# mLSTM heads in pairs on TensorE, with four weight and decay buffers and a finish spread over two batches

## The reference

```python
h_in = rmsnorm(x, norm1_w)
q, k, v = heads(h_in @ wq), heads(h_in @ wk), heads(h_in @ wv)   # 8 heads, 16 / 16 / 32 features
o_pre = h_in @ w_og
i_pre, f_pre = soft_cap(h_in @ w_ig + b_ig), soft_cap(h_in @ w_fg + b_fg)
Fcum = cumsum(log_sigmoid(f_pre))
Dmat = where(causal, Fcum[s] - Fcum[t] + i_pre[t], -inf);  m = max_t(Dmat)
C = (q @ k.T / sqrt(16)) * exp(Dmat - m)
n = max(|sum_t C|, exp(-m));  h = (C / n) @ v                    # for each head
h_out = sigmoid(o_pre) * (h * rsqrt(mean(h * h) + eps) * mh_w)
x1 = x + h_out @ w_out
out = x1 + silu(rmsnorm(x1) @ w_gate) * (rmsnorm(x1) @ w_up) @ w_down
```

## Time and profile before

| | |
|---|---|
| median of three runs | 750.72 us |
| the profiled execution | 753.29 us |
| its span | 751.5 us |
| PE busy | 712.5 us (95%), mean granted clock 0.935 |
| DVE busy | 443.5 us (59%) |
| ACT busy | 423.5 us (56%) |
| POOL busy | 252.0 us (34%) |

### The profile page before, as it was taken

How to read it: one execution, slowest core, us unless ns; L and a number is a source line. 1 busy time by engine, 2 the same in 40 slices (tenths; PEclk the granted TensorE clock), 3 DMA queues, 4 the chain that set the end, 5 groups by cost and what they waited for, 6 DMA issues and landing times. The chain is left out here.

```text
span 751.5 us, 15356 instructions
## 1 busy us (share of the span) xinstructions
PE 712.5 (95%) x5290; PEld 670.3 (89%) x5290; DVE 443.5 (59%) x961; ACT 423.5 (56%) x1106; POOL 252.0 (34%) x265
## 2 busy tenths in 40 slices
PE   8999999999999999999987999988998799999995
PEld 8999999999999999999877999987666579999995
DVE  6465665576655766566565655643155437655686
ACT  5566686667756677666684333366454544333553
POOL 3624742244422434224741411217254122111011
PEclk9999999999999999999999999998556659999998
DMA  6266644456343663436500400007320100000000
GB/s 228 72 209 196 174 131 123 119 167 176 118 119 100 181 181 102 131 96 185 169 3 4 159 2 0 15 11 235 113 69 15 44 0 1 2 0 0 1 28 28
DMA packets 44889, 69.63 MB, mean 93 GB/s; under 512 B 3376, under 2 KB 30640, under 8 KB 44592
## 3 DMA queue, kind: packets, MB, share of 16 engines
q1 hardware_dynamic: 44416, 68.31, 30.4%
q10 hardware_dynamic: 432, 0.79, 0.3%
HBM read 52.18 MB, written 16.91 MB: 92 GB/s over the span
## 5 line engine op out<-in xcount | busy, mean ns | idle before, releaser
L303 PE MATMUL PJ<-xTh,WBh 128*128 128x256 f32 x364 | 106.6, 293 | 0.4 <-POOL WBl L808 0.4
L305 PE MATMUL PJ<-xTh,WBl 128*128 128x256 f32 x364 | 102.7, 282 | 0.0
L304 PE MATMUL PJ<-xTl,WBh 128*128 128x256 f32 x364 | 102.7, 282 | 0.0
L545 ACT ACTIVATE probs<-SC,nmax 128x256 f32<-128x256 f32 x128 | 59.5, 471 | 63.9 <-DVE nmax L671 62.4
L793 POOL TENSOR_TENSOR stage<-stage 128x256 f32<-128x256 f32 x32 | 24.5, 765 | 164.1 <-DVE stage L659 164.1
L669 DVE TENSOR_REDUCE rmax<-SC 128x2 f32<-128x512 f32 x64 | 44.2, 691 | 54.4 <-PE SC L384 47.5
L1154 PE MATMUL UG<-xTh,WBh 128*128 (+1 forms) x256 | 73.5, 287 | 1.1 <-PEq L49 1.1
L552 ACT ACTIVATE probs<-probs,rinv 128x256 f32<-128x256 f32 x128 | 58.5, 509 | 27.2 <-DVE rinv L675 27.1
L1157 PE MATMUL UG<-xTh,WBl 128*128 (+1 forms) x256 | 72.4, 283 | 0.0
L1155 PE MATMUL UG<-xTl,WBh 128*128 (+1 forms) x256 | 72.4, 283 | 0.0
L303 PEld LDWEIGHTS PJ<-xTh,WBh 128*128 128x128 f32 x364 | 69.2, 190 | 1.0 <-issue 0.6
(11 more groups left out here) (252 smaller groups left out, 2453.4 us busy)
## 6 DMA issues: line engine op xcount, KB each, us to landing
K<-scr_k SPq DMA_DIRECT2D x60, 256.0 KB, 4.5
raw<-in_w_att SPq DMA_DIRECT2D x37, 256.0 KB, 4.7
Q<-scr_q SPq DMA_DIRECT2D x15, 512.0 KB, 7.4
stage<-scr_m SPq DMA_DIRECT2D x4, 1024.0 KB, 5.9
scr_q<-rot_h SPq DMA_DIRECT2D x30, 128.0 KB
scr_q<-rot_l SPq DMA_DIRECT2D x30, 128.0 KB
scr_k<-rot_h SPq DMA_DIRECT2D x30, 128.0 KB
scr_k<-rot_l SPq DMA_DIRECT2D x30, 128.0 KB
```

The source lines that it names most:

```text
L303: pe.matmul(out, ah, bh, start=(i == 0), stop=False)
L304: pe.matmul(out, ah, bl, start=False, stop=False)
L305: last = pe.matmul(out, al, bh, start=False, stop=(i == n - 1))
L545: last = act.activation(probs[:, j % 2, t, :], SC[j % 2][:, t, :], ACT.Exp, scale=SCALE, bias=nmax[:, j % 2, t:t + 1], accum_out=rsum[:, j ...
```

## The change

- The loop over heads becomes a loop over pairs (`PAIRS`). PE issues the scores of two heads together, one pair ahead, across batches too, and then the values of two heads together.
- Decays and weights have four buffers each instead of two. The two new ones of each kind lie in `rows`, a tile that also holds the rows of the gates (`cumS`, `gr`, `nm`, `ones`, `M`), which are dead by then. The first values therefore wait for the last output gate. ACT runs four heads ahead of the weighing.
- `rows_T` goes ahead of the last projection, and `exp_nm` and the first four decays between the parts of the last evacuation. The mask of batch 0 is added by DVE in quarters of two heads (`mask_first`) instead of by POOL; two of them stand behind the first two weighings. All weight pieces of the feed-forward are split in batch 0, and SP loads them ahead of the rows of batch 2.
- The finish of batch c is spread over batches c + 1 (to `norm_b`) and c + 2 (`heads_T`, `project_out`, `add_heads`), the norm over c + 2 and c + 3. The rest goes into the first two batches of the feed-forward, whose second batch is written out for that (`finish_last`).
- The output gate is `tanh(o / 2)`, and `norm_b` multiplies by `1 + tanh(o / 2)`, twice the sigmoid. The factor 4 in `norm_a` takes the 2 back.

```diff
-        cumS, gr, M, nm, ones = (sb(n, [P, S]) for n in ("cumS", "gr", "M", "nm", "ones"))
+        rows = sb("rows", [P, 6 * S])
+        cumS, gr, nm, ones, M = (rows[:, i * S:(i + 1) * S] for i in range(5))
...
+        decay_buf = [ga[:, 0, :], ga[:, 1, :], rows[:, 768:1152], rows[:, 1152:1536]]
+        weight_buf = [gb[:, 0, :], gb[:, 1, :], rows[:, 0:384], rows[:, 384:768]]
...
+            if second_hook:
+                chunk(1, False)
+            with eng.Fori(2 if second_hook else 1, B) as c:
...
-        AT = dict(take=0, squares=2, norm_a=2, norm_b=4, heads_T=5, hoT_hi=7, hoT_lo=7, out=7,
-                  ssq=3, xs=3, T=4, hi=5)
-        MLP_PIECES = (3, 2, 2)
+        PAIRS = HM // 2
+        MLP_PIECES = (2, 2, 2, 1)
...
                 pe.wait_ge(s_["c_ready"], HM * c + h + 1)
+                if c == 0 and h == 0:
+                    pe.wait_ge(s_["og_ready"], TT * B)
                 if c or h >= 4:
                     pe.wait_ge(s_["vt_ready"], HM // 2 * c + h // 2 - 1)
-                w = gb[:, h % 2, :]
+                w = weight_buf[(HM * c + h) % 4]
...
-                scores(c, 0)
-                for h in range(HM):
-                    if h + 1 < HM:
-                        scores(c, h + 1)
-                    values(c, h)
-                    if h == 0 and c:
-                        back(c - 1, 3)
-                    if h in (2, 4, 6):
-                        back(c, h // 2 - 1)
-                    if h == AT["T"] and c >= 2:
-                        pe_T(pe, 2, c - 2)
-                    if h == AT["heads_T"] and c:
-                        heads_T(c - 1)
-                    if h == AT["out"] and c:
-                        project_out(c - 1)
+                if c == 0:
+                    scores(0, 0)
+                    scores(0, 1)
+                for pair in range(PAIRS):
+                    if pair + 1 < PAIRS:
+                        scores(c, 2 * pair + 2)
+                        scores(c, 2 * pair + 3)
+                    elif c + 1 < B:
+                        scores(c + 1, 0)
+                        scores(c + 1, 1)
+                    values(c, 2 * pair)
+                    values(c, 2 * pair + 1)
+                    if pair:
+                        back(c, pair - 1)
+                    elif c:
+                        back(c - 1, PAIRS - 1)
+                    if pair == 0 and c >= 2:
+                        heads_T(c - 2)
+                    if pair == 0 and c >= 3:
+                        pe_T(pe, 2, c - 3)
+                    if pair == 1 and c >= 2:
+                        project_out(c - 2)
...
             for c in range(1, B):
                 project(c)
-            rows_T()
+                if c == 2:
+                    rows_T()
             for c in range(B):
...
             def finish_heads(k, c, ht):
                 if ht == 0:
-                    back(3, 3)
+                    back(3, PAIRS - 1)
+                    heads_T(2)
+                if ht == 1:
+                    project_out(2)
+                    pe_T(pe, 2, 1)
+                if ht == 5:
+                    heads_T(3)
+                if ht == 6:
+                    project_out(3)
+                    pe_T(pe, 2, 2)
+            def finish_last(ht):
                 if ht == 2:
-                    pe_T(pe, 2, 2)
-                if ht == 4:
-                    heads_T(3)
-                if ht == 5:
-                    project_out(3)
-                if ht == 7:
                     pe_T(pe, 2, 3)
-            ffn_pe(pe, 1, finish_heads)
+            ffn_pe(pe, 1, finish_heads, finish_last)
...
-                    act.activation(og_v[:, c, t, :], UG[2 + t][:, D:2 * D], ACT.Sigmoid).then_inc(s_["og_ready"], 1)
+                    act.activation(og_v[:, c, t, :], UG[2 + t][:, D:2 * D], ACT.Tanh, scale=0.5).then_inc(s_["og_ready"], 1)
...
-                if h % 4 == 0:
-                    act.wait_ge(s_["masked"], 2 * c + h // 4 + 1)
-                if c or h >= 2:
-                    act.wait_ge(s_["c_ready"], HM * c + h - 1)
-                e, a, at = ga[:, h % 2, :], A[c % 2], 32 * c + h
+                if c == 0 and h % 2 == 0:
+                    act.wait_ge(s_["masked_first"], h // 2 + 1)
+                if c and h % 4 == 0:
+                    act.wait_ge(s_["masked"], 2 * (c - 1) + h // 4 + 1)
+                if c or h >= 4:
+                    act.wait_ge(s_["c_ready"], HM * c + h - 3)
+                e, a, at = decay_buf[(HM * c + h) % 4], A[c % 2], 32 * c + h
...
+            exp_nm()
             mlp_hi(4, 5)
-            evac(3)
-            exp_nm()
+            evac_qk(3)
+            decay(0, 0)
+            decay(0, 1)
+            evac_og(3)
+            decay(0, 2)
+            decay(0, 3)
             for c in range(B):
-                for h in range(HM):
-                    decay(c, h)
-                    if h == 0 and c:
-                        take_pair(c - 1, 3)
-                    if h in (3, 5, 7):
-                        take_pair(c, (h - 3) // 2)
-                    if h == AT["take"] and c:
+                for pair in range(PAIRS):
+                    if pair:
+                        take_pair(c, pair - 1)
+                    elif c:
+                        take_pair(c - 1, PAIRS - 1)
+                    if pair == 0 and c >= 2:
+                        hoT(c - 2)
+                    if pair == 0 and c >= 3:
+                        act_hi(act, 2, c - 3)
+                    if pair == 1 and c:
                         take(c - 1)
-                    if h == AT["squares"] and c:
                         squares(c - 1)
-                    if h == AT["ssq"] and c >= 2:
+                    if pair == 2 and c >= 2:
                         act_ssq(act, 2, c - 2)
-                    if h == AT["hi"] and c >= 2:
-                        act_hi(act, 2, c - 2)
-                    if h == AT["hoT_hi"] and c:
-                        hoT(c - 1)
-                    if c < 3 and h >= 8 - MLP_PIECES[c]:
-                        i = 5 + sum(MLP_PIECES[:c]) + h - 8 + MLP_PIECES[c]
-                        mlp_hi(i, i + 1)
-            take_pair(3, 3)
+                    if c == 0:
+                        i = RING + sum(MLP_PIECES[:pair])
+                        mlp_hi(i, i + MLP_PIECES[pair])
+                    for u in (HM * c + 2 * pair + 4, HM * c + 2 * pair + 5):
+                        if u < HM * B:
+                            decay(u // HM, u % HM)
...
+            def mask_first(quarter):
+                dve.wait_ge(a_in[0], 32)
+                a = A[0][:, 2 * quarter:2 * quarter + 2, :].rearrange("p h (b n) -> p h b n", n=P)[:, :, 0:3:2, :]
+                m = mask[:, :].rearrange("p (a b n) -> p a b n", a=1, b=1).broadcast_to([P, 2, 2, P])
+                dve.tensor_tensor(a, a, m, ALU.add).then_inc(s_["masked_first"], 1)
...
-                if c or h >= 2:
-                    dve.wait_ge(s_["pv_ready"], HM * c + h - 1)
-                dve.scalar_tensor_tensor(gb[:, h % 2, :], UG[h % 2][:, 0:384], 1.0 / math.sqrt(DQ), ga[:, h % 2, :],
+                u = HM * c + h
+                if u >= 4:
+                    dve.wait_ge(s_["pv_ready"], u - 3)
+                dve.scalar_tensor_tensor(weight_buf[u % 4], UG[h % 2][:, 0:384], 1.0 / math.sqrt(DQ), decay_buf[u % 4],
...
-                dve.tensor_tensor(ho[:, :, :], ho[:, :, :], og_v[:, c, :, :], ALU.mult).then_inc(s_["ho_ready"], 1)
+                dve.scalar_tensor_tensor(ho[:, :, :], og_v[:, c, :, :], 1.0, ho[:, :, :], ALU.add,
+                                         ALU.mult).then_inc(s_["ho_ready"], 1)
...
             split(1)
             split(2)
-            split(3)
             dve.wait_ge(s_["rows_ready"], 1)
             dve.tensor_copy(gcol[:, :, :], X[:, 0:S].rearrange("p (t h) -> p t h", t=TT)).then_inc(s_["gcol_ready"], 1)
+            split_qk(3)
+            mask_first(0)
+            take_v(3, 0)
+            mask_first(1)
+            take_v(3, 1)
             for c in range(B):
-                for h in range(HM):
-                    weigh(c, h)
-                    if h == AT["norm_a"] and c:
+                for pair in range(PAIRS):
+                    weigh(c, 2 * pair)
+                    weigh(c, 2 * pair + 1)
+                    if c == 0 and pair == 0:
+                        mask_first(2)
+                        mask_first(3)
+                    if pair == 0 and c >= 2:
+                        hoT(c - 2)
+                    if pair == 0 and c >= 3:
+                        dve_lo(dve, 2, c - 3)
+                    if pair == 1 and c:
                         norm_a(c - 1)
-                    if h == AT["xs"] and c >= 2:
+                    if pair == 2 and c >= 2:
+                        add_heads(c - 2)
+                    if pair == 3 and c:
+                        norm_b(c - 1)
+                    if pair == 3 and c >= 2:
                         dve_xs(dve, 2, c - 2)
...
```

(17 more changed lines are left out.)

102 lines of the change are left out of this document (55 added, 47 removed).

## The result

The changed kernel takes 720.34 us (median of 4 runs, 716.76 to 721.65), the kernel before 750.81 (749.76 to 752.95): ratio 0.958, 95% interval 0.954 to 0.963. 711 was forecast, range 703 to 731. So the direction and the wide range held; the forecast's own range of 704 to 718 did not, and rival 1's 722 is nearest by number, though not by mechanism, as the clock shows.

A forecast was written before the change was run, and what follows sets the result against it. PE at half clock with little idle bounds the head stage; feed-forward at 576.2 instead of 619.98 saves 43.8, less 2.4 moved: 753.3 - 41.4 = 711.9 profiled, 709.3 median, plus 2 for stalls: 711 us, range 703 to 731.

The forecast's parts named there:

- rival 1: Head stage: the clock rises only with the first projection, then holds; median 722 us; chance 0.23.
- Pairs: PE in the head stage: two heads' scores overlap, 1.13 us instead of 2.08, saving 11.4 us over four batches at 1.2 GHz.
- The clock rises by itself in batch 0: Head stage: dense pairs lift PE's clock to full at about 531, without a projection, after two low pairs of 4.48 us.
- Four buffers remove the idle time and hold the clock: Head stage: weighing runs beside the previous pair's values, so 10.4 us of PE idle should go and the clock stays up.
- The lock at the start: Batch 0: two quarter masks on DVE wait for POOL's mask at the shared port; 0 to 4.8 us lost, 3.2 taken.
- the price of nothing for the mask of batch 2: SyncE's queue: weight pieces now ahead of batch 2's rows cost nothing, as rows and mask are needed only after batch 1 begins.
- the terms of 11.5 us for batch 1 and 14 for each of the last two: Head stage at high clock: batch lengths, ending at 548.2 after batch 1 and 576.2 after batches 2 and 3.
- Rival 4: DVE and POOL port: blocked DVE instructions make PE wait, twelve costing 29 us; slower, median 762 us; chance 0.03.
- The transposed heads: DVE's finish work between pairs: its slot is about 1.3 us per pair at high clock; 2 us added for PE stalls.
- ScalarE's pace: Later batches of the head stage: ACT needs 13.3 us, PE at high clock 9.9 and about 2.4, so 13.3 at least.
- 2: Second rival, head stage: the clock rises with projections and falls again, or stays low; 723 to 733, middle 728 us; chance 0.20.
- 3: Third rival, PE's scores: the pairs don't overlap, taking 11.4 us back at low clock; median 745 us at most; chance 0.05.

The follow-up runs named there:

- e5: Changed kernel with PE alternating one head's scores and one head's values instead of two and two: 731.85 us, ratio 0.974 to the kernel before.
- p1: Kernel before with only the order in pairs added (scores of two heads, then values of two heads): 749.88 us, ratio 0.997.
- e7: Changed kernel with the sigmoid gate and its table load again, first decays behind the last gates: 719.98 us, ratio 0.957 to the kernel before.
- e4: Changed kernel with two decay and two weight buffers instead of four: 721.45 us, ratio 0.958 to the kernel before.
- e2: Changed kernel with the masks of batches 2 and 3 added on VectorE as quarter masks instead of on GpSimd: 719.03 us, ratio 0.957 to the kernel before.
- e6: Changed kernel with the mask of batch 0 on GpSimd again, without the four quarter masks on VectorE: 714.25 us, ratio 0.951 to the kernel before.
- e1: Changed kernel with the causal masks of batches 2 and 3 left out: 715.64 us, ratio 0.952 to the kernel before.
- e8: Changed kernel with GpSimd's masks of batches 1 to 3 in four instructions of half the size instead of two: 715.97 us, ratio 0.954 to the kernel before.
- e3: Changed kernel with VectorE's low parts of the transposed heads behind the weighings of pair 1 instead of ahead: 717.21 us, ratio 0.951 to the kernel before.
- b1: Changed kernel with e6, e8 and e3 together, and ScalarE's part of the transposed heads also in pair 1: 707.78 us, ratio 0.942 to the kernel before.
- b2: b1 with the norm's first half on VectorE behind the weighings of pair 2 instead of ahead: 706.40 us, ratio 0.939 to the kernel before.

## Why the prediction was right or wrong

*Pairs.* Right, and more than it said. Two heads' scores take 0.61 us at full rate and 1.05 at half (against 1.13 estimated), and the order in pairs keeps the clock up: its undoing cost 11.5 us (e5). What the prediction did not see is that this holds only together with the rest of the change: alone it brought 1.6 us (p1).

*The clock rises by itself in batch 0.* In the changed kernel it never fell there: the start was better than forecast (PE waits 0.64 us for the first weights, 2.93 before), so batch 1's first values began at 533.50, not 536.7, although this execution reached the heads 1.7 us later than the one before did. Where the start was spoilt, the rise came without a projection as forecast, but later: after some 14 us of low clock in e7 and 17 in p1, instead of 10. The Trainium skill, TensorE: Matmul & The Clock Gate, section What's actually happening, says that activity releases the half rate; e5's 26 busy microseconds at 0.50 bear out that the busy share of the records does not tell when.

*Four buffers remove the idle time and hold the clock.* Wrong: e4 has the same waits and the same clock with two. What is left of idle time is waits for the norm, the transposed heads and the masks, and those are the same with two buffers and with four.

*The lock at the start.* 3.2 us were taken for it; two quarter masks took 3.45 instead of 2 x 0.68, so 2.1 us, and 4.2 in e2's execution. That is 1.7 and 2.8 us each, on the side of the sign named for the lock (2 us each, under 0.8 against it). But they did not have to be blocked at all (e6).

*The step that failed* is the price of nothing for the mask of batch 2, and with it the terms of 11.5 us for batch 1 and 14 for each of the last two. The expected sign, decays that wait for a mask, was the wrong one. The mask was in time for them and met the norm of batch 0 on VectorE, with the weighings behind it in order. The moved weight pieces themselves held the rows back by 1.6 us at most, and no run puts them back, so it is open whether the old order on SyncE's queue would have missed the norm. From first values to first values batch 1 took 553.54 - 533.50 = 20.0 us, batches 2 and 3 took 586.79 - 553.54 = 33.3 instead of 28. That is 8.5 + 5.3 late, 3.2 early, together the 10.6 by which the feed-forward started later than 576.2. In e1, without the late masks, batch 1 took 545.56 - 531.50 = 14.1 us and the last two 575.45 - 545.56 = 29.9: the mask accounts for 6.0 of the 8.5 us, the rest of batch 1 is mostly the wait behind the norm, and for 3.4 of the last two, which begin at half clock behind it. That is the one profiled execution, 11 us shorter; in the medians e1 is 2 to 5 us lower, and how much of the time is the mask's doing stays open between these.

Rival 4 had this mechanism, with PE waiting at many places; it acted at two, 1.74 us at the start and 4.97 in batch 1, the latter with a clock at half for 17. The Trainium skill, SBUF — State Buffer, section Who interferes with whom, says that of the two the one that issues second waits until the other's instruction is done; e8 agrees, with 0.54, 1.19 and 1.19 us beside instructions of 1.24, where 1.58 and 2.27 stood beside ones of 2.4.

*The transposed heads.* Their order on VectorE the prediction saw as a slot of 1.3 us per pair and priced at 2 us in all. e3 takes the last two batches from 33.3 to 582.80 - 553.58 = 29.2 us, again in one execution.

*ScalarE's pace.* The prediction held that a batch at high clock lasts 13.3 us at least, from what ScalarE did in one before. In b1 batch 2 takes 561.21 - 548.59 = 12.6 us with ScalarE busy for 10.86, and batch 3 takes 11.6. The 13.3 counted two weight pieces of 0.63 us, which the change itself had moved to batch 0; where the rest went was not followed up. So 14 for each was too long, and in the changed kernel the waits hid it. That the forecast missed by 10 us only is partly luck: this and the earlier start stand against the waits that it left out.

*Rivals 1 to 3.* 1 is refuted: the clock was full without a projection in 524 to 537, and after its fall at about 540 it rose near 557, ahead of the first projection at 564.05. The head transposes, also of full size, stand at that place (556.62), but in e7 the clock rose at about 537 with neither. 2 had one thing right: the clock falls again, during the longest wait and after each of the two others. Its reason, values and scores that leave too much of the array idle, is not enough by itself, since the clock holds through 25 us of them in b2, where transposes and projections stand among them, and through 13 us in the changed kernel (524 to 537), where they do not. 3 falls with the scores' rows.

*The moved finish.* From the first feed-forward matmul to the end of the span: 133.0 us instead of 131.5, 1.5 more where 2.4 were added.

## What to carry to other kernels

Where a step is moved on one queue, ask not only who waits for its result but what it will run beside: a GpSimd instruction on SBUF data can hold even a tiny VectorE instruction, and everything in order behind it, for its whole length; keep such instructions short, or away from VectorE's small links. Put what feeds TensorE ahead of everything that waits for another engine's round trip. And undo the parts of a change singly: here the order in pairs carried 11.5 of some 30 us, the four buffers and the tanh gate with its earlier decays nothing measurable, the masks on VectorE cost some 2 to 6, and the pairs were worth almost nothing alone.

## What the runs showed of the hardware

- A quarter of a microsecond of alignment goes with 2.1 us: two equal VectorE instructions took 1.36 us alone, 3.45 when they began 0.38 us before GpSimd's, 3.44 when they began 0.14 before (e1), 5.58 when they began 0.10 after (e2). Weighing, which reads PSUM beside SBUF, took 1.01 us for two at 523.76, in the middle of GpSimd's mask.
- The granted clock can stay at 0.50 for 26 us in which the records show PE busy all the time, and rise among the same kinds of matmuls in another order (e5 and e7).
- Waits of PE of 2.31 and 2.65 us were each followed by 3.4 us at half clock; 1.63 + 0.22 and 1.92 + 0.28 (e3) were not, yet 1.31 in b2 was (0.51 in 543.5 to 547). The same wait at the same place in batch 2 (2.30 us) was followed by full clock in e1, e6 and e8. So the length of a wait alone does not tell whether the clock falls; what does is open, and with it a part of what each edit above gained.
